# All of a half's scores in one slot, one split of the weights per turn, and a third exponential buffer

## The reference

```python
def step(carry, seg):
    mem, z = carry
    qq, kk, vv = seg
    sigma_q = jax.nn.elu(qq) + 1.0
    scores = jnp.einsum('bhsk,bhtk->bhst', qq, kk) / scale
    scores = jnp.where(causal_mask, scores, -jnp.inf)
    att_dot = jax.nn.softmax(scores, axis=-1) @ vv
    att_mem = sigma_q @ mem / (sigma_q @ z)
    sigma_k = jax.nn.elu(kk) + 1.0
    delta = vv - sigma_k @ mem / (sigma_k @ z)
    mem_new = mem + jnp.einsum('bhsk,bhsv->bhkv', sigma_k, delta)
    z_new = z + sigma_k.sum(axis=-2, keepdims=True).transpose(0, 1, 3, 2)
    att = beta * att_mem + (1.0 - beta) * att_dot
    out = att.reshape(Bsz, SEG, H * DV) @ Wo
    return ((mem_new, z_new), out)
```

## Time and profile before

| what | value |
|---|---|
| median of 3 runs | 704.97 us (703.26 to 705.03) |
| profiled execution | 700.46 us, its span on the core 698.7 us |
| busy share of the span | PE 90%, PEld 79%, DVE 58%, ACT 47%, POOL 45% |
| mean granted TensorE clock | 0.973 of full speed |
| the eight stages of `delta_attention` | from 36.62 to 427.9 us of the span |
| GpSimd's split operations | L449 x84 of 675 ns, L453 x84 of 815 ns |
| loads of Wq, Wk, Wv | 8, 8 and 8 of 512 KB |

### The profile page before, as it was taken

How to read it: one execution, slowest core, us unless ns; L and a number is a source line. 1 busy time by engine, 2 the same in 40 slices (tenths; PEclk the granted TensorE clock), 3 DMA queues, 4 the chain that set the end, 5 groups by cost and what they waited for, 6 DMA issues and landing times. The chain is left out here.

```text
span 698.7 us, 12315 instructions
## 1 busy us (share of the span) xinstructions
PE 631.6 (90%) x4182; PEld 549.8 (79%) x4182; DVE 404.2 (58%) x1047; ACT 331.5 (47%) x812; POOL 311.3 (45%) x379
## 2 busy tenths in 40 slices
PE   3888999999999999999999998698999958996897
PEld 3767888988988988988988998586777746985675
DVE  6849387287297286296295463786233259636444
ACT  3646766467467468468467563322344312201221
POOL 4775463552552652452551020515777514301474
PEclk9999999999999999999999999899999979997899
DMA  8111101110110110210200042496333253008641
GB/s 265 38 37 56 31 31 31 32 48 21 58 28 17 59 39 0 65 32 0 69 1 1 25 97 68 163 412 201 104 102 100 79 186 120 0 1 297 230 122 45
DMA packets 29777, 57.89 MB, mean 83 GB/s; under 512 B 4670, under 2 KB 15904, under 8 KB 29728
## 3 DMA queue, kind: packets, MB, share of 16 engines
q1 hardware_dynamic: 22720, 42.03, 17.8%
q0 software_dynamic: 4896, 13.12, 6.6%
q10 hardware_dynamic: 2112, 2.10, 0.9%
HBM read 48.06 MB, written 10.09 MB: 83 GB/s over the span
## 5 line engine op out<-in xcount | busy, mean ns | idle before, releaser
L919 DVE RECIPROCAL denominators<-readings 128x2 f32<-128x2 f32 x120 | 19.8, 165 | 133.1 <-PE readings L591 132.1
L449 POOL TENSOR_TENSOR w_high<-xn,ones 128x256 fp32r<-128x256 f32 x84 | 54.1, 675 | 82.4 <-PE ahead L235 46.9
L798 ACT ACTIVATE memory_reading<-readings,denominators 64x128 f32<-64x128 f32 x240 | 73.6, 356 | 12.2 <-DVE denominators L919 10.5
L591 PEld LDWEIGHTS readings<-memory_copy,sigma 128*128 128x128 f32 x480 | 70.3, 191 | 10.9 <-ACT memory_copy L789 3.4
L591 PE MATMUL readings<-memory_copy,sigma 128*128 128x129 f32 x480 | 74.0, 276 | 2.0 <-ACT memory_copy L789 1.7
L601 PE MATMUL memory<-minus_delta,sigma_k_tokens 128*128 128x129 f32 x480 | 73.5, 275 | 0.0
L925 DVE SCALAR_TENSOR_TENSOR minus_delta<-readings,denominators,v 64x128 f32<-64x128 f32 x224 | 69.0, 348 | 4.0
L774 ACT ACTIVATE x<-ahead 128x512 f32<-128x512 f32 x60 | 35.8, 597 | 72.0 <-PE ahead L235 38.2
L789 ACT ACTIVATE memory_copy<-memory 128x258 f32<-128x258 f32 x120 | 47.1, 393 | 48.1 <-PE memory L601 48.1
L1229 POOL DMA_INDIRECT xs_e<-rows_e,gather_at_e x46 | 44.6, 969 | 50.7 <-DVE gather_at_e L1643 18.8
L453 POOL TENSOR_TENSOR w_low<-xn,w_high 128x256 fp32r<-128x256 f32 x84 | 65.9, 815 | 1.6
(11 more groups left out here) (285 smaller groups left out, 1424.8 us busy)
## 6 DMA issues: line engine op xcount, KB each, us to landing
weights_e<-experts SPq DMA_DIRECT2D x24, 608.0 KB, 12.0
xn<-L_attn_Wq SPq DMA_DIRECT2D x8, 512.0 KB, 4.0
xn<-L_attn_Wk SPq DMA_DIRECT2D x7, 512.0 KB, 3.8
xn<-L_attn_Wv SPq DMA_DIRECT2D x7, 512.0 KB, 3.9
wo<-L_attn_Wo SPq DMA_DIRECT2D x1, 2048.0 KB, 13.2
rows_e<-xn ACTq DMA_DIRECT2D x4, 512.0 KB, 8.1
x<-L_attn_x SPq DMA_DIRECT2D x4, 256.0 KB, 3.5
x<-L_attn_x SPq DMA_DIRECT2D x2, 512.0 KB, 3.8
```

The costliest lines, as they stand in the source:

```text
L449: last = pool.tensor_tensor(w_high[i][:, :, of], w_stage[:, :, of], one, ALU.mult)
L591: last = pe.matmul(KQ[g][:, hh * MC:(hh + 1) * MC], sqk[:, GROUP * g + hh, pair, 2 * par:2 * par + 2, :], mz[g][:, hh, :], start=True, sto ...
L798: last = act.activation(read[rows, half, GROUP * g + hh, pair, :], KQ[g][rows, hh * MC:hh * MC + DK], ACT.Copy, scale=nr[g][rows, hh:hh + 1])
```

## The change

- `qT` and `kT` hold one half's queries and keys, and share one tensor; both calls of `scores` stand at slot 0, the second in PSUM bank `L[1]`. The softmax tiles `sm`, `mx`, `ssum`, `rs` are doubled. The masks stand at VectorE's slots 1 and 2, the exponentials at ScalarE's slots 4 and 6, the sums at VectorE's slots 6 and 10.
- The turned readings move from slots 1 to 4 to slots 2 to 5, the additions with them; `turn_sigma_k` of the four heads moves from slots 7 to 10 to slots 8 to 11.
- The weights have three buffers and are split once a turn, in its first half: Wq behind the first probabilities, Wk and Wv behind the second.
- The exponentials of the projections go through three buffers in place of two.
- The table `place` gets a tensor of its own and is loaded at the start. The split of the first Wv no longer waits for a projection.

```diff
-        qT, kT = carried.space, sb("kT", [P, HQ, T])
+        qT, kT = carried.space[:, :, 0:HALF], carried.space[:, :, HALF:T]
-        sm = sb("scores", [P, NT, SEG])
+        sm = [sb(f"scores{i}", [P, NT, SEG]) for i in range(2)]
-        AHEAD_AT = {u: [("project", u)] for u in range(7)}
-        AHEAD_AT |= {7: [("project", 7), ("turn", 0)], 8: [("turn", 1), ("project", 8)],
-                     9: [("turn", 2), ("project", 9)], 10: [("turn", 3), ("project", 10)], 11: [("project", 11)]}
+        AHEAD_AT = {u: [("project", u)] for u in range(8)}
+        AHEAD_AT |= {8 + h: [("turn", h), ("project", 8 + h)] for h in range(HQ)}
-        READINGS_AT = {1: 0, 2: 1, 3: 2, 4: 3}
-        READINGS_BANK = (1, 0, 1, 0)
+        READINGS_AT = {2: 0, 3: 1, 4: 2, 5: 3}
+        READINGS_BANK = (0, 1, 0, 1)
...
-                def stage(n, first=False, value_weights=True, key_weights=True):
...
+                def split_next(it, i):
+
+                    pool.wait_ge(proj_ready, 24 * it + 16 + 4 * i)
+                    split(i, 3 * it + 4 + i)
+                    pool.wait_ge(low_done, 3 * it + 4 + i)
+
+                def turn(it, first, last):
+                    for half in range(2):
+                        n, before = 2 * it + half, not (first and not half)
+                        if before:
+                            pool.wait_ge(p_ready, 4 * n)
+                        for pp in range(2):
+                            shift_scores(n, pp)
+                        pool.wait_ge(shifted, 2 * n + 2)
+                        probabilities(n, 0, before)
+                        if not (half or last):
+                            pool.wait_ge(p_ready, 4 * n + 2)
+                            split_next(it, 0)
+                        probabilities(n, 1)
+                        if not (half or last):
+                            pool.wait_ge(p_ready, 4 * n + 4)
+                            split_next(it, 1)
+                            split_next(it, 2)
...
-                pool.wait_ge(proj_ready, 4)
-                split(0, 3, 1)
+                pool.wait_ge(low_done, 2)
+                split(2, 3, 1)
...
                     if m == 0:
-                        if behind:
-                            pe.wait_ge(bt_copied, 4 * n - 1)
-                        scores(n, half, 0)
-                    if m == 6:
-                        if behind:
-                            pe.wait_ge(att_ready, 4 * n)
-                        pe.wait_ge(masked, 2 * n + 1)
-                        scores(n, half, 1)
+                        for pp in range(2):
+                            if behind:
+                                pe.wait_ge(bt_copied, 4 * n - 1 + pp)
+                            scores(pp)
...
                     if m == 8:
                         pe.wait_ge(p_ready, 4 * n + 2)
-                        pe.wait_ge(masked, 2 * n + 2)
+                        if behind:
+                            pe.wait_ge(att_ready, 4 * n)
+                        else:
+                            pe.wait_ge(masked, 2 * n + 2)
...
-                        if u >= 2:
-                            act.wait_ge(sigma_ready, 8 * n + u - 1)
-                        act.activation(e[u % 2][:, :], bank[:, :], ACT.Exp)
+                        if u >= 3:
+                            act.wait_ge(sigma_ready, 8 * n + u - 2)
+                        act.activation(e[u % 3], bank[:, :], ACT.Exp)
...
-                    if m in (4, 9):
-                        exp_scores(n, m // 8)
+                    if m in (4, 6):
+                        exp_scores(n, m // 6)
...
-                    if m in (1, 7):
-                        mask_scores(2 * n + m // 7, behind or m == 7)
-                    if m in (5, 10):
-                        sum_exp(2 * n + m // 10)
+                    if m in (1, 2):
+                        mask_scores(n, m - 1, behind)
+                    if m in (6, 10):
+                        sum_exp(n, m // 10)
```

More of the change, by code:

```diff
@@ L267, in delta_attention @@
         xh, xl = norm.xh, norm.xl
-        w_high = [sb(f"w_high{i}", [P, KD, HQ * DK], F32R) for i in range(2)]
-        w_low = [sb(f"w_low{i}", [P, KD, HQ * DK], F32R) for i in range(2)]
+        w_high = [sb(f"w_high{i}", [P, KD, HQ * DK], F32R) for i in range(3)]
+        w_low = [sb(f"w_low{i}", [P, KD, HQ * DK], F32R) for i in range(3)]
         w_staged = norm.xn[1][:, 0:TPH, :].rearrange("p t d -> p (t d)").rearrange("p (k n) -> p k n", k=KD)
@@ L391, in _ @@
                 sp.dma_start(wo[:, :, :], Wo.rearrange("(i p) n -> p i n", p=P)).then_inc(wo_loaded, 16)
-                load_weights(Wq, 0, 1)
-                load_weights(Wk, 0, 4)
+                sp.dma_start(place[:, :, :], place_in).then_inc(place_loaded, 16)
                 def turn(it, first, last):
-                    load_weights(Wv, it, 6 * it + 5)
+                    if not last:
+                        load_weights(Wq, it + 1, 3 * it + 3)
                     if not first:
@@ L399, in turn @@
                     if not last:
[L400 to L402 removed]
+                        load_weights(Wk, it + 1, 3 * it + 4)
+                        load_weights(Wv, it + 1, 3 * it + 5)
                     if not first:
                         store_out(it - 1, 1, 2 * it - 1)
[L405 to L407 removed]
                 all_turns(sp, turn)
@@ L508, in _ @@
                 pool.wait_ge(low_done, 1)
                 split(1, 2, 0)
-                pool.wait_ge(proj_ready, 4)
-                split(0, 3, 1)
+                pool.wait_ge(low_done, 2)
+                split(2, 3, 1)
                 pool.wait_ge(low_done, 3)
                 set_constants()
-                pool.wait_ge(proj_ready, 12)
-                split(0, 4)
-                split(1, 5)
-                stage(0, True)
-                with pool.Fori(0, STAGES - 3) as i:
-                    stage(i + 1)
@@ L520, in _ @@
-                stage(STAGES - 2, False, True, False)
-                stage(STAGES - 1, False, False, False)
+                all_turns(pool, turn)
                 norm.invert(pool, 1, 0)
@@ L537, in wait_copied, with project @@
                         pe.wait_ge(v_copied, u - 7)
-                def project(n, half, u, free=None, at_start=None):
+                def project(n, half, u, turn, free=None, at_start=None):
                     b = A[PROJECT_BANK[u]] if at_start is None else at_start
@@ L544, in project @@
                     if u % 4 == 0:
-                        pe.wait_ge(low_done, 3 * n + u // 4 + 1)
+                        pe.wait_ge(low_done, 3 * turn + u // 4 + 1)
                     if at_start is not None:
@@ L603, in update_memory, with scores @@
                     last.then_inc(upd_ready[g], 1)
-                def scores(n, half, pp):
+                def scores(pp):
                     for s in range(STEPS):
@@ L609, in scores @@
                             h, pair, par = GROUP * pp + hh, s // 2, s % 2
-                            seg = slice((half * STEPS + s) * SEG, (half * STEPS + s + 1) * SEG)
+                            seg = slice(s * SEG, (s + 1) * SEG)
                             at = (hh * TPH + pair) * SEG
-                            last = pe.matmul(L[0][par * SEG:(par + 1) * SEG, at:at + SEG], qT[:, h, seg], kT[:, h, seg],
+                            last = pe.matmul(L[pp][par * SEG:(par + 1) * SEG, at:at + SEG], qT[:, h, seg], kT[:, h, seg],
                                              start=True, stop=True)
@@ L691, in slot @@
                                 free = (skt_copied, 4 * n + 4) if first else (y_copied, n - 1)
[L692 removed]
+                            project(n + 1, 1 - half, u, it + half, free)
                     out_at = OUT_AT if ahead else LAST_OUT_AT
```

96 lines of the change are left out of this document (37 added, 59 removed).

## The result

| | before | after |
|---|---|---|
| median of 9 runs each | 704.07 us (701.47 to 706.76) | 698.71 us (696.97 to 699.73) |
| ratio to before | | 0.9921 [0.9901, 0.9941] |
| first profiled execution | 700.46 us | 698.28 us |

The change makes the kernel faster by 0.8%: 5.4 us, by the interval 4.2 to 7.0. The forecast was no change. The pair of profiles differs by 2.2 us only, so two questions follow: what the profiles' difference is made of, and where the other 3 us are.

What follows compares the result with a forecast made beforehand. TensorE was taken to set the pace, except from slot 2 to slot 8, where it follows VectorE. -1.4 - 5.8 + 4.6 + 2.7 = +0.1 us, on a median of 704.97, gave 705.0; range 697.5 to 710.

Steps and rivals of the forecast that it cites:

- Stages 1 to 6, +0.77 each: Middle stages: scores to `turn_probs` 25.14 us against 24.72, +0.42, and `turn_sigma_k(0)` moved behind it, +0.35; +4.6 for six.
- the first rival: Stages only rename their wait: chain 0.77 us shorter a stage than added up, stage 7 unchanged; 697.8 us, chance 0.20.
- The capping beside the shift: VectorE's capping beside GpSimd's second shift in slot 3: taken as 0.63 us against 0.43, adding 0.20 to the chain.
- The keys turned behind `turn_probs`: `turn_sigma_k(0)` leaves slot 7 for behind `turn_probs`, where TensorE has no wait: +0.35 us a stage.
- the last rival: Split of next Wq slows VectorE's keys sigmas in slots 7 and 8: 2.5 us in stages 0, 2, 4; 712.5, chance 0.12.
- Stage 0, -5.8: Stage 0: scores to `turn_probs` 21.98 us against 28.16, without the 2.83 wait for a split, and 0.35 behind it.
- Start, -1.4: Before the first scores: GpSimd's 1.58 us wait ahead of the split of Wv is removed; bounds 0 and -1.58.
- Stage 7, +2.7: Last stage: with a second scores call ahead, `turn_probs` comes 17.27 us after the scores against 14.53; bounds 0 and +2.9.
- GpSimd's slack: Splits once a turn cost nothing because GpSimd has slack; were it gone, `turn_probs` of slot 12 would wait for Wq's split.

## Why the prediction was wrong

**The sum had its terms in the right places and three of them too dear.** -1.4 - 5.8 + 4.6 + 2.7 was +0.1. The rows give -6.6 + 1.7 + 2.1 behind the start, and the start is worth between 1.2 and 3.2, by what one takes for it (below): -4.0 to -6.0, measured -5.4 [-7.0, -4.2].

- *Stages 1 to 6, +0.77 each: the largest error.* That the wait would be renamed, from VectorE's mask to GpSimd's multiplication behind a gapless VectorE chain, is what the rows show. The chain was 0.67 us shorter: the step of slot 2 at 6.02 for 6.34, since the reading ahead of it stands at 5.38 for 5.69 (the second scores call adds 0.93 and not 1.13, and the turned reading that left was worth 0.46 and not 0.35); VectorE to the sum 15.13 for 15.39, for in slots 4 and 5 a step took 0.72 and a sigma 1.06, where I had 0.86 and 1.19; to GpSimd 1.04 for 1.12. `turn_probs` stands at 24.47, so scores to `turn_probs` is 0.25 shorter than before instead of 0.42 longer. I added start-to-start distances of other places as if each were exact; six times 0.67 is 4.0 us, near what I had written down as the first rival. The capping beside the shift took 0.63 (141.19), the value I chose.
- *The keys turned behind `turn_probs`:* +0.36 to +0.38 in stages without a split, as costed (0.35).
- *The split of the next Wq*, the last rival: its mechanism is there at a fifth of its price. Stages 0, 2 and 4 pay 0.5 us each, as the profile without splits shows, and not 2.5; the sum had this term at nothing. The second key's sigma took 0.75, 1.11 and 0.84 beside the split and 0.41, 0.69 and 0.43 without it. The rule of the Trainium skill that I cited, page "SBUF — State Buffer", section "Who interferes with whom", has the second instruction blocked until the first has finished. The trace agrees in direction: each of these operations grew, by 0.34 to 0.42, while one of the split's took 0.71 to 0.97 (2.82 and 3.86 for four). Only one of the three has two inputs in SBUF, as the rule that I cited wants; the capping and the copy have one, and grew as much. So at most the rest of one is waited out, about half, and not the 0.73 each that I took from a row beside the multiplications.
- *Stage 0, -5.8:* -6.6 against three profiles. `turn_probs` stands at 21.08 for 21.98, again the shorter chain, and 0.5 us behind it go to the split of Wq.
- *Start, -1.4:* 1.2 between profiles of the quick pace, 1.4 with the wait put back, 2.2 between profiles of the slow pace (23.89 and 21.7), but 3.2 in the timed runs, or 2.4 at a like mean clock. So the timed runs lose about what the slow pace costs, and some clock; which pace they had is not recorded, and no profile shows a fall behind the wait of 1.96.
- *Stage 7, +2.7:* +2.1. The first mask stands at 3.54 for 3.74, `turn_probs` at 16.58 for 17.27.

That the loads and the third exponential buffer cost nothing fits the rows: no wait of TensorE in the stages names them. GpSimd's slack, which I took as large enough, is so only with the splits in one half: with three in every half, stages 1 to 6 took 5.3 us more, 3.2 of it by the clock.

## What to carry to other kernels

Where a chain is put together from distances measured elsewhere and used many times over, a tenth of a microsecond in each link decides the sign: price the link from the place nearest to the new one, and let the range of the sum grow with its count. Look for idle time of the engine that sets the chain just ahead of it: two masks moved into VectorE's idle 3 us were worth as much as the whole change. A wait at the start that is visible for 2 us in one profile may cost more in other executions, so put it back by itself and time it, and set runs of like granted clock side by side.

## What the runs showed of the hardware

In the stages of this layer the granted clock fell to the lower level only behind waits of TensorE, each time for some 3.4 us: behind 2.83 us of idling in stage 0 of the kernel before (40.46 to 43.87, and alike in its other profiles), and with the weights' part undone behind 1.91 and behind 1.54 and 0.79 in stage 0 and behind 0.75 and 1.03, the second beginning 1.5 us behind the first, in stages 3 and 5. There it cost 1.6 us a time, more than either wait; yet the same two waits went without a fall in stages 1, 2 and 4, and 0.44 and 0.94 in the changed kernel in all of them. Once it fell in stage 7, behind 0.62, 0.60 and 0.97 (keys a slot earlier, splits late), waits that every other profile has there without a fall. What tells these apart was not found.

One and the same start ran at matmuls 0.23 or 0.43 us apart from execution to execution. The trace's first entry of the granted clock, at the full level, stands at 12.3 to 13.9 us in the quick ones, ahead of the first projection, and at 18.1 to 19.7 in the slow ones, where the distance changes. What decides when the clock rises was not found.

Of the 22 executions of the kernel before beside one group of experiments, the quickest took 697.91 us at a mean granted clock of 0.975, and the one with the lowest, 0.958, took 707.50.
